# Copying the input into the output by DMA during attention, and adding the gated product onto it with accumulating stores

## What is computed

```python
    x = L0_attn_x
    xn = _layernorm(x, axis=-1)
    s = _L0_attn_ref(xn, L0_attn_Wq, L0_attn_Wk, L0_attn_Wv, L0_attn_Wo)
    g = _silu(_L0_ffn_ref(xn, L0_ffn_gate_w, L0_ffn_w_gate_up, L0_ffn_w_down, L0_ffn_shared_gate_up, L0_ffn_shared_down))
    x = x + s * g
    return x
```

## Time and profile before

| what | us |
|---|---|
| median of 3 runs (lowest, highest) | 739.17 (738.39, 739.94) |
| the profiled execution | 737.62 |
| its span in the profile | 735.7 |
| busy in the span: PE, DVE, POOL, ACT | 659.1, 581.6, 537.8, 442.3 |
| attention's last projection on DVE (L1121) begins | 572.4 |
| the last load-back of results (L501) is issued | 707.6 |
| the last sum on DVE (L1268) ends | 733.2 |

### The profile page before, as it was taken

The page is one execution under the profiler, slowest core; times in us unless marked ns, Lnnn a source line. Parts: engine busy times, 40 slices in busy tenths (PEclk is TensorE's granted clock), DMA queues, the critical chain, the costliest instruction groups (busy, mean ns, idle before and its releaser), DMA issues.

```text
span 735.7 us, 17233 instructions
## 1 busy us (share of the span) xinstructions
PE 659.1 (90%) x4994; PEld 460.8 (63%) x4995; DVE 581.6 (79%) x1683; ACT 442.3 (60%) x1205; POOL 537.8 (73%) x588
## 2 busy tenths in 40 slices
PE   3678869789999999999999999999987899999992
PEld 1255546556766667676666766667665577767761
DVE  6988879789999999998999999999876344333378
ACT  3585636465657666575675657668584664555542
POOL 4677777978888887888877888888988993555510
PEclk9899989999999999999999999999998999999996
DMA  9491000500000000000000000000122564665772
GB/s 306 165 301 48 1 0 2 141 22 16 0 14 14 0 14 0 14 7 7 14 0 14 0 14 14 0 14 2 35 70 88 167 117 105 138 141 138 210 285 101
DMA packets 64952, 50.44 MB, mean 69 GB/s; under 512 B 35252, under 2 KB 58260, under 8 KB 64916
## 3 DMA queue, kind: packets, MB, share of 16 engines
q1 hardware_dynamic: 60804, 39.45, 19.3%
q0 software_dynamic: 3840, 10.52, 4.3%
q10 hardware_dynamic: 272, 0.02, 0.0%
HBM read 24.72 MB, written 18.96 MB: 59 GB/s over the span
## 4 chain that ended last, share of the span: by engine, by line
POOL 41%; issue 19%; PE 17%; DVE 13%; ACT 7%; DMA 2%; POOLq 0%; SPq 0%; DVEq 0%
POOL arena L539 16%; PE bank L1546 8%; POOL arena L533 8%; POOL arena L526 7%; PE bank L1576 6%; POOL xs_dram L586 4%; ACT arena L777 3%; POOL compare L582 2%; PE bank L1555 2%; DVE arena L1108 2%; POOL arena L563 1%; ACT arena L785 1%; DVE arena L1082 1%; DVE arena L1083 1%; DVE arena L1078 1%
## 5 line engine op out<-in xcount | busy, mean ns | idle before, releaser
L539 POOL TENSOR_TENSOR arena<-arena,rinv 128x128 f32<-128x128 f32 (+3 forms) x256 | 176.4, 720 | 83.5 <-DVE rinv L1102 83.4
L777 ACT ACTIVATE arena<-bank,nmax 128x512 f32<-128x512 f32 (+3 forms) x256 | 132.5, 535 | 64.6 <-DVE nmax L1096 64.6
L1096 DVE CUSTOM_DVE_ANT_0 bank<-bank,mask_b 128x512 f32<-128x512 f32 (+3 forms) x256 | 118.1, 516 | 14.2 <-issue 14.2
L1390 PE MATMUL bank<-arena 128*128 128x512 f16 (+7 forms) x768 | 116.4, 302 | 5.9 <-POOL arena L533 5.9
L785 ACT CAST arena<-bank 128x512 f16<-128x512 f32 (+1 forms) x192 | 93.3, 522 | 45.1 <-PE bank L1403 43.5
L1359 PE MATMUL bank<-xnT_hi,arena 128*128 (+1 forms) x320 | 111.0, 389 | 9.2 <-DVE arena L1083 4.7
L1419 PE MATMUL bank<-arena 128*128 128x512 f16 (+7 forms) x768 | 118.0, 305 | 0.0
L1403 PE MATMUL bank<-ident_f,arena 128*128 128x128 f32 x640 | 93.5, 277 | 25.5 <-DVE arena L1108 14.5
L1108 DVE TENSOR_TENSOR arena<-bank,arena 128x512 bf16<-128x512 f32 (+1 forms) x192 | 109.0, 595 | 3.9 <-ACT arena L785 1.8
L526 POOL TENSOR_TENSOR arena<-arena 128x512 f32<-128x512 f32 x77 | 98.6, 1281 | 2.5 <-DVE arena L1083 2.2
L1403 PEld LDWEIGHTS bank<-ident_f,arena 128*128 128x128 f32 x640 | 74.0, 142 | 38.9 <-DVE arena L1108 18.3
(11 more groups left out here) (147 smaller groups left out, 1158.9 us busy)
## 6 DMA issues: line engine op xcount, KB each, us to landing
xs_dram<-s_sb SPq DMA_DIRECT2D x4, 1548.0 KB, 14.4
stage<-w_gate_up SPq DMA_DIRECT2D x16, 352.0 KB
arena<-ys_dram SPq DMA_DIRECT2D x8, 512.0 KB, 6.5
stage<-w_down SPq DMA_DIRECT2D x16, 176.0 KB
stage<-wq SPq DMA_DIRECT2D x4, 512.0 KB, 8.0
stage<-wo SPq DMA_DIRECT2D x4, 512.0 KB, 6.5
stage<-x SPq DMA_DIRECT2D x1, 2048.0 KB, 10.6
out<-s_sb SPq DMA_DIRECT2D x8, 256.0 KB, 2.1
```

The lines of the kernel that those rows point to most:

```text
L539: ins = pool.tensor_tensor(pr, pr, rinv[:, par, qt:qt + 1].to_broadcast([P, (qt + 1) * P]), ALU.mult)
L777: ins = act.activation(probs[par][:, P_AT[qt]:P_AT[qt] + n], score_bank[u][:, col:col + n], ACT.Exp, scale=-1.0, bias=nmax[:, par, qt:qt + ...
L1096: ins = dve.tensor_tensor_reduce(score_bank[u][:, col:col + n], score_bank[u][:, col:col + n], mask_b[:, S - n:S], -1.0, 3e38, ALU.add, AL ...
L1390: ins = pe.matmul(score_bank[u][:, col:col + n_k], qT[a][:, j * S + qt * P:j * S + (qt + 1) * P], kT[m][:, 0:n_k], start=(n == 0), stop=(n ...
```

## The change

- The load of `x` back into `stage` (L492) and the wait for it on DVE are gone, with the view `x_back`.
- A DMA that copies all of `x` to `out` (2048 KB, DRAM to DRAM) stands in SP's program behind the loads of the shared expert and ahead of the first routed expert. It increments the semaphore `x_again`.
- `finish(g)` on DVE is the multiplication alone. The wait for its own product, the addition, and the semaphore `summed` are gone.
- The eight stores move from SP to POOL, behind its 48 indirect DMAs. POOL waits for the copy once, and then per group for the product. Each store has `accum_op=ALU.add`: the DMA adds the 256 KB of the group onto what stands in `out`.
- SP still ends the program after the eight stores' landing.

```diff
-        x_back = stage[:, 0:NT * D].rearrange("p (t d) -> p t d", d=D)
...
+            sp.dma_start(out.rearrange("b s d -> (b s) d"), x.rearrange("b s d -> (b s) d")).then_inc(x_again, 16)
+
             for e in range(E_ROUTED):
...
-            sp.wait_ge(expert_low, E_ROUTED)
-            sp.dma_start(x_back, x_t).then_inc(x_again, 16)
...
-            out_t = out.rearrange("b (t p) d -> p (b t) d", p=P)
-            for g in range(GROUPS):
-                sp.wait_ge(summed, g + 1)
-                t = slice(g * BACK, (g + 1) * BACK)
-                sp.dma_start(out_t[:, t], s_sb[:, t.start * D:t.stop * D].rearrange("p (t d) -> p t d", d=D)).then_inc(stored, 16)
             sp.wait_ge(stored, 16 * GROUPS)
...
+            out_t = out.rearrange("b (t p) d -> p (b t) d", p=P)
+            pool.wait_ge(x_again, 16)
+            for g in range(GROUPS):
+                pool.wait_ge(gated, g + 1)
+                t = slice(g * BACK, (g + 1) * BACK)
+                pool.dma_start(out_t[:, t], s_sb[:, t.start * D:t.stop * D].rearrange("p (t d) -> p t d", d=D),
+                               accum_op=ALU.add).then_inc(stored, 16)
...
-                    dve.wait_ge(x_again, 16)
                 dve.wait_ge(gate_act, g + 1)
                 dve.tensor_tensor(s_sb[:, cols], s_sb[:, cols], y_sb[:, cols], ALU.mult).then_inc(gated, 1)
-                dve.wait_ge(gated, g + 1)
-                s = s_sb[:, cols].rearrange("p (t d) -> p t d", d=D)
-                dve.tensor_tensor(s, s, x_back[:, ffn_rows(g), :], ALU.add).then_inc(summed, 1)
```

More of the change, by code:

```diff
@@ L348, in build @@
         x_again = sem("x_again")
-        pair_sum, ffn_sum, gate_act, gated, summed, stored = sem("pair_sum"), sem("ffn_sum"), sem("gate_act"), sem("gated"), sem("summed"), sem("stored")
+        pair_sum, ffn_sum, gate_act, gated, stored = sem("pair_sum"), sem("ffn_sum"), sem("gate_act"), sem("gated"), sem("stored")
         PASSES = ((0, 0), (0, 1), (1, 0))
```

## The result

The changed kernel is slower. The ratio of its time to that of the kernel before is 1.0048, with a 95% interval of 1.0033 to 1.0063: about 3.5 us more. The medians are 743.11 us (13 runs) and 738.62 us (13 runs); they lie 4.5 us apart, the means of the same runs 3.5. The forecast was 2.5 us less.

What follows compares the result with a forecast made beforehand. DVE was taken to bound the end section. 5.8 us saved there less 3.3 given back by POOL's stores gave 739.17 - 2.47 = 736.7 us; range 735.0 (rival 1, cheap stores) to 741.0.

Steps and rivals of the forecast that it cites:

- DVE is the limit of the end, and 5.76 us are saved there: End section: DVE saturated from 714 us; dropping eight additions saves 0.72 us each, 5.76 us in all.
- ACT and PE keep their slack: End section: with DVE earlier, ACT's last gate keeps 0.47 us and PE's projection path 0.85 us.
- Issue on POOL, 1.29 us: Each adding store takes POOL 1.29 us to issue, taken from indirect DMAs; bounds 0.96 to 2.23 us.
- Rival 2: POOL's store issue goes by rows, 2.23 us each, so the last stores queue: 740.4 us; chance 0.14.
- Landing, 3.75 us, and the rate, at most 2.1 us per store: Adding stores land 3.75 us after issue, about 1.0 for the read; engines need 1.4 to 2.1 us per store.
- Rival 3: DMA engines add much more slowly than they copy, 2.8 us per store, so stores pile up: 743.7 us; chance 0.11.
- The span ends 0.4 us after the last landing: Program end: last store lands at 732.83 us and the span ends 0.4 us later, at 733.2.
- The sum: End section: 5.8 us saved on DVE, 3.3 given back by stores (1.65 POOL queue, 1.65 longer landing), net 2.5 us less.
- The copy of `x` and the load that goes: Attention copy hidden, taking 5 or 10 us; removing the load at 690.5 counted as 0 us.

Runs made afterwards that it cites:

- e1_sp_plain: Changed kernel with its eight stores back on SP, plain, without adding the input; ratio 0.9933 to the kernel before, end section 26.2 us.

## Why the prediction was wrong

- **DVE is the limit of the end, and 5.76 us are saved there.** Right: 29.2 against 23.5 us, 5.7 us, with no idle time on DVE from 712 on; and with the stores left plain on SP the whole of it reaches the time (4.9 us by the ratio, 5.5 by the section).
- **ACT and PE keep their slack.** Right: no wait for them appears on DVE in the part that became shorter. The last gate ended in time for the last three multiplications to follow each other.
- **Issue on POOL, 1.29 us.** Right in size (1.2, three in 3.64 us), but by luck: it was taken from an indirect DMA, and a direct store costs 0.71 us plain and 1.2 only with the addition. Rival 2's 2.23 us per store didn't occur.
- **Landing, 3.75 us, and the rate, at most 2.1 us per store.** Mis-sized, and by itself enough to undo the gain. Without the addition a store lands in 2.5 us, near my 2.75; the read and the addition, which I took at 1.0 us, go with 2.0 more. A store alone so lands in 4.5 us, the last of the burst in 7.2. The engines need 2.2 us per store, a little more than the three full passes that I took as the extreme. I had 1.29 us between the stores of the burst, hidden in the issues; the last three landings (at about 733.7, 736.4 and 737.7) lie 2.0 us apart on average. So the last landing came 7.8 us after DVE's last result and not 5.4 (732.83 less 727.44). With the 0.4 us of before behind it the span would have ended at 738.1, and the section would have been 31.7 us long, as in the kernel before. Rival 3, which asked for a slow rate, was right about the direction: its mark, DMA slices that are busy throughout, is there. But it decides from 2.3 us and the rate is 2.2, so the stores don't pile up before the burst (the fifth still lands in 4.3 us). That its 743.7 us are near the measured time is luck.
- **The span ends 0.4 us after the last landing.** This is the step that failed in its mechanism, where the landing was wrong only in its size. It was read from the earlier trace rows, a store on SP, and carried over to POOL. POOL's program then ends late: its DRAIN ends 6.6 to 7.3 us after its last instruction (8.6 after the burst of adding stores). The kernel before has that row too; it was hidden, and I hadn't looked at what the engines do behind their last instruction. In the changed kernel the span ends 3.8 us after the last landing and not 0.4, and even plain stores leave no gain once they are on POOL (1.0010).
- **The sum.** Forecast 5.8 us saved and 3.3 given back. Measured: 5.7 saved and 9.1 given back (11.6 less 2.5). By the experiments the move from SP to POOL costs 5.7 us by the ratios and 6.0 by the sections, of which some 5 are DRAIN (from 731.3, 0.4 us behind the last landing, to 736.4) and the rest is POOL's issue and landing. The adding costs 2.8 us by both. It costs less than its landing says, because part of it lies beside DRAIN.
- **The copy of `x` and the load that goes.** Right: 0.9994 for the copy alone. It landed in 8.8 to 11.1 us in the five profiles that have all of it, so the slower of my two values, 10 us, was the better one. Without the load at 690 (e1_sp_plain) the section is shorter by 5.5 us, no more than DVE's saving, so counting 0 for it was right.

My range ended at 741.0, just past rival 2, and left rival 3 out. No rival had the mechanism that decided.

**What stays open.** What DRAIN does in its time isn't shown, and so not whether anything in the kernel can shorten it. Why it ends 8.6 us after the last issue behind the burst of adding stores, and 6.6 to 7.3 in all other cases, wasn't settled; and whether it would be shorter in a kernel whose POOL issues no DMA at all wasn't tried.

## What to carry to other kernels

Read the last instructions of every engine, not only of the one that ends last: what an idle-looking engine pays when its program ends becomes visible as soon as it is given the last piece of work. Here the last thing that POOL does should be over some 7 us before the last store lands; a store that has to be late belongs on SP's queue. And an adding DMA is not a store with a free addition: it saved DVE 0.72 us per 256 KB and cost the DMA engines 1.6 us. Four of them, issued one by one ahead of the last burst, left a small gain (0.9979); all eight, three of them in the burst, a loss (1.0048).

## What the runs showed of the hardware

- POOL's DRAIN at the end of the program ended 6.6 us (last instruction an indirect DMA), 6.65 (a plain store), 6.7 (an addition), 7.0 (a single adding store), 7.25 us (three plain stores) after POOL's last instruction, and took 7.26 us with every DMA landed; only behind three adding stores in a row it ended 8.6 us after. The same instruction takes 0.66 us on ACT, 0.73 to 1.15 on DVE and 0.01 on SP:

```profile
L186 ACTq DRAIN  x1: 661/661/661, 728.2 to 728.2; - x1
L186 DVEq DRAIN  x1: 1149/1149/1149, 728.9 to 728.9; - x1
...
L186 SPq DRAIN  x1: 13/13/13, 737.8 to 737.8; - x1
```

- A store of 256 KB by POOL: plain 0.71 us to issue, 2.5 to land, 0.65 of the DMA engines; adding 1.2, 4.5 and 2.2 us.
- A copy of 2 MB from DRAM to DRAM, with the experts' loads behind it in the queue, took 8.8 to 11.1 us in five profiles (10.5 us are 200 GB/s of payload), and its cost in attention didn't show in the time (0.9979 to 1.0008).
- An addition of POOL with both inputs in SBUF made DVE's instruction of the same kind end 0.5 us after it, instead of running beside it: 1.39 us instead of 0.68. A copy from PSUM beside it kept its 0.41 us.
